# The bonus term of an RWKV layer as a block-diagonal matmul, in a kernel with a written-out order on every engine

## The reference

```python
r = xrg @ Wr.T
k = k * jnp.exp(w * mk)            # k, v, w, kk, a come from low-rank mixes of x
_, y = jax.lax.scan(step, s0, (qt, wt, kt, vt, at, bt))      # the state, token by token
y = ((yg - mu) / jnp.sqrt(var + EPS)).reshape(Bx, Tx, C) * ln_w + ln_b
# the bonus: one number for each token and head, times the head's values
rk = (r.reshape(Bx, Tx, H, HS) * k.reshape(Bx, Tx, H, HS)
      * time_faaaa.reshape(H, HS)).sum(-1, keepdims=True)
y = y + (rk * v.reshape(Bx, Tx, H, HS)).reshape(Bx, Tx, C)
return y * g @ Wo.T
```

## Time and profile before

| | before |
|---|---|
| time, median of 3 runs | 3364.82 us (3361.93 to 3368.27) |
| profiled execution: its own time | 3367.22 us |
| its span, first to last instruction | 3365.5 us |
| granted TensorE clock, mean | 0.977 |
| TensorE busy / weight loads | 2931.0 / 2550.6 us |
| VectorE busy | 2887.9 us |
| ScalarE busy | 1831.5 us |
| GpSimd busy | 1444.6 us |

### The profile page before, as it was taken

One profiled execution on the slowest core, in us unless ns is written; L12 is line 12 of the kernel. 1 busy time (PEld: TensorE's weight loads), 2 busy tenths in 40 slices (PEclk: granted clock), 3 DMA queues, 4 the chain that ended last, 5 costly groups with the idle time before them and its releaser, 6 DMA issues.

```text
span 3365.5 us, 175696 instructions
## 1 busy us (share of the span) xinstructions
PE 2931.0 (87%) x80128; PEld 2550.6 (76%) x80128; DVE 2887.9 (86%) x5699; ACT 1831.5 (54%) x3457; POOL 1444.6 (43%) x1224
## 2 busy tenths in 40 slices
PE   6898888998888989888888888888988889888895
PEld 5777777787777777777777777777777778777774
DVE  4888898898898888898888988888888889889885
ACT  3555564564554555655555645555556556555452
POOL 5344344444353444444443543534434435435332
PEclk8999999999999999999999999999999999999997
DMA  3121221221211212212212212122122122122121
GB/s 115 46 60 38 53 56 36 58 55 36 60 46 45 60 37 53 59 38 53 56 38 56 52 39 60 39 52 60 37 53 56 38 56 56 38 56 48 43 53 36
DMA packets 92604, 170.69 MB, mean 51 GB/s; under 512 B 13908, under 2 KB 14932, under 8 KB 91864
## 3 DMA queue, kind: packets, MB, share of 16 engines
q1 hardware_dynamic: 91864, 159.45, 19.8%
HBM read 41.97 MB, written 16.78 MB: 17 GB/s over the span
## 4 chain that ended last, share of the span: by engine, by line
PE 63%; DVE 27%; issue 8%; DMA 1%; POOL 0%; ACT 0%; SPq 0%; POOLq 0%; DVEq 0%; ACTq 0%
PE bank L1101 22%; PE bank_a L1240 11%; PE bank L1301 8%; DVE stacked L938 4%; PE bank_a L1218 3%; PE bank_b L1218 3%; PE bank_b L1271 3%; DVE kt L859 3%; PE bank_a L1256 3%; PE bank_a L1248 2%; DVE x2n L985 2%; PE bank_b L1291 2%; DVE xm_rg L815 2%; DVE xm_k L815 2%; DVE xm_v L815 2%
## 5 line engine op out<-in xcount | busy, mean ns | idle before, releaser
L474 POOL TENSOR_TENSOR rs<-rs,minus_half 128x1 f32<-128x1 f32 x64 | 35.0, 548 | 1168.1 <-DVE rs L981 1168.1
L676 ACT ACT_TABLE_LOAD x256 | 328.4, 1283 | 4.6
L1240 PE MATMUL bank_a<-pw,w_ffn_int 32*32 32x64 f32 x16384 | 273.3, 216 | 57.3 <-issue 50.7
L1101 PEld LDWEIGHTS bank<-xm_k,w_k 128*128 128x128 f32 x2048 | 236.4, 194 | 107.8 <-issue 107.8
L1101 PE MATMUL bank<-xm_k,w_k 128*128 128x128 f32 x2048 | 246.6, 279 | 79.1 <-DVE xm_rg L815 77.4
L1101 PEld LDWEIGHTS bank<-xm_v,w_v 128*128 128x128 f32 x2048 | 269.6, 204 | 58.8 <-issue 53.1
L1240 PEld LDWEIGHTS bank_a<-pw,w_ffn_int 32*32 32x32 f32 x16384 | 242.9, 106 | 82.9 <-issue 60.4
L1101 PE MATMUL bank<-xm_v,w_v 128*128 128x128 f32 x2048 | 288.0, 291 | 14.2 <-issue 14.1
L1301 PE MATMUL bank<-w_o,yc 128*128 128x512 f32 x512 | 285.9, 663 | 9.3 <-DVE yc L780 9.3
L1101 PE MATMUL bank<-xm_rg,w_r 128*128 128x128 f32 x2048 | 257.6, 279 | 0.8 <-issue 0.7
L1101 PEld LDWEIGHTS bank<-xm_rg,w_r 128*128 128x128 f32 x2048 | 239.1, 192 | 8.2 <-issue 2.3
(11 more groups left out here) (198 smaller groups left out, 8621.9 us busy)
## 6 DMA issues: line engine op xcount, KB each, us to landing
streamed<-aq_state SPq DMA_DIRECT2D x128, 384.0 KB
streamed<-w_ffn_int SPq DMA_DIRECT2D x128, 384.0 KB, 5.3
xin<-in_x SPq DMA_DIRECT2D x128, 128.0 KB
xres<-in_x SPq DMA_DIRECT2D x128, 128.0 KB
out<-o_sb SPq DMA_DIRECT2D x128, 128.0 KB, 2.4
w_ffn_int<-in_weight_q SPq DMA_DIRECT2D x1, 2048.0 KB, 10.7
w_k<-in_Wk SPq DMA_DIRECT2D x1, 1024.0 KB
w_r<-in_Wr SPq DMA_DIRECT2D x1, 1024.0 KB
```

The source lines that it names most:

```text
L676: nc.scalar.preload_act_table_set(functions)
L1101: ins = mm(bank[:, o * n:(o + 1) * n], weights[:, k, o * P:(o + 1) * P], x[:, k].rearrange("p b t -> p (b t)"), start=(k == 0), stop=(k == ...
L1240: ins = mm(bank_a[q, 64 * n:64 * n + 64], pt[q, g, :], source[q, g, 0:2].rearrange("p j t -> p (j t)"), start=True, stop=True)
```

## The change

`w_bonus` is a 128 x 128 matrix for each block of channels, block-diagonal with four 32 x 32 blocks, each row filled with the channel's `time_faaaa`. TensorE multiplies it with `qk`, which sums over the channels of a head and spreads the sum over them in one go, into `fb[3]`; VectorE multiplies that with `val`. `bonus_rows`, `bonus_sums` and the transposition in `bonus` on VectorE, `weighted_bonus` and `bonus_values` on GpSimd are gone. New waits: `values` on ScalarE for `v_rkv` (tile before), `transposed_input` on TensorE for `v_rkv` (it writes `fb[3]`), TensorE's `bonus` for `g_qk` and `a_mk`, GpSimd's `bonus` for `p_bonus`, VectorE's `undecayed` for `a_a`. All four compute engines have a new order; SyncE's is unchanged.

```diff
@@ constants, GpSimd and VectorE
+                then(pool.memset(w_bonus[:], 0.0))
+                for h in range(QH):
+                    then(pool.memset(w_bonus[quad(h), :, quad(h)], 1.0))
...
-            V.transpose(faaaa_T[:], faaaa[:].unsqueeze(2).to_broadcast([P, KB, HS])).then_inc(ffn_done, 1)
             dve.wait_ge(masks_done, 1)
+            for k in range(KB):
+                ins = V.tensor_scalar(w_bonus[:, k], w_bonus[:, k], faaaa[:, k:k + 1], None, ALU.mult)
+            ins.then_inc(ffn_done, 1)
@@ ScalarE
             def values(i):
                 act.wait_ge(p_v, count(i, 1, 1))
                 act.wait_ge(v_vraw, count(i, 1, 0))
+                act.wait_ge(v_rkv, count(i, 1, 0))
@@ VectorE
             def bonus(m):
-                dve.wait_ge(g_rkv, count(m, 1, 1))
+                dve.wait_ge(p_bonus, count(m, 1, 1))
+                dve.wait_ge(a_v, count(m, 1, 1))
                 dve.wait_ge(g_z3, count(m, 1, 0))
-                V.transpose(by_chunk(rkv), qkT[:]).then_inc(v_rkv, 1)
+                tt(rkv[:], fb[3][:], val[:], ALU.mult).then_inc(v_rkv, 1)
@@ TensorE
             def transposed_input(i):
                 pe.wait_ge(a_xn, count(i, 1, 1))
                 pe.wait_ge(a_mk, count(i, 1, 0))
+                if i >= 2:
+                    pe.wait_ge(v_rkv, count(i - 2, 1, 1))
...
+            def bonus(m):
+                pe.wait_ge(g_qk, count(m, 1, 1))
+                pe.wait_ge(a_mk, min(count(m + 1, 1, 1), NT))
+                for k in range(KB):
+                    ins = mm(fb[3][:, k * TOK:(k + 1) * TOK], w_bonus[:, k],
+                             qk[:, k * B * NC:(k + 1) * B * NC].rearrange("p g t -> p (g t)"), start=True, stop=True)
+                ins.then_inc(p_bonus, 1)
```

More of the change, by code:

```diff
@@ L726, in tile_step @@
                 if project:
-                    mk_gate(i)
                     tables(EXP_LN)
+                    log_squares(i)
+                if solve:
+                    power(m, 1)
+                if project:
                     log_sigmoid(i)
[L730 to L734, removed]
                     exponentials(i)
@@ L737, in tile_step @@
                     normalised(j)
+                if solve:
+                    value_pairs(m)
+                    power(m, 2)
+                if mix:
                     front_transposed(j)
                 if project:
+                    key_decay(i)
                     values(i)
+                    queries(i)
+                if mix:
+                    tables(SIGMOID_TANH)
+                    low_rank(j)
                 if solve:
@@ L852, in undecayed @@
             def undecayed(i):
+                dve.wait_ge(a_a, count(i, 1, 1))
                 dve.wait_ge(g_kkp, count(i, 1, 1))
@@ L1034, in tile_step @@
                 if solve:
-                    bonus(m)
-                    power(m, 2)
-                if project:
-                    removal_directions(i)
+                    power(m, 1)
                 if mix:
@@ L1041, in tile_step @@
                 if solve:
-                    half_inverse(m)
-                    right_hand_sides(m, 0)
+                    bonus(m)
+                if project:
+                    removal_directions(i)
+                if solve:
+                    power(m, 2)
                 if project:
@@ L1351, in tile_step @@
                     half_inverse(m)
-                    from_values_and_state(m, 0)
-                if mix:
-                    transposed_input(j)
-                if solve:
-                    inverse(m)
                 if finish:
                     project_out(n, [2])
+                    project_out(n, [3])
                 if project:
@@ L1361, in tile_step @@
                 if solve:
-                    solve_step(m, 0)
-                if finish:
-                    project_out(n, [3])
+                    inverse(m)
+                if mix:
+                    low_rank(j)
                 if project:
@@ L1367, in tile_step @@
                 if solve:
+                    solve_step(m, 0)
+                    output_gate(m)
                     from_solutions(m, 0)
-                if mix:
-                    low_rank(j)
-                if solve:
-                    output_gate(m)
-                    from_values_and_state(m, 1)
                 if mix:
@@ L1376, in tile_step @@
                 if solve:
-                    solve_step(m, 1)
+                    from_values_and_state(m, 1)
                 if finish:
```

138 lines of the change are left out of this document (63 added, 75 removed).

## The result

The changed kernel took 3283.45 us at the median of four runs (3277.99 to 3293.85), the kernel before 3363.38 us beside it: ratio 0.9768, 95% interval 0.9737 to 0.9798. That is 80 us less, where 30 were forecast; it lies in the range, at its fast edge.

A forecast was written before the change was run, and what follows sets the result against it. TensorE (87% busy) and VectorE (86%) were too close to name one; each step chains a stretch of both. 38.7 + 2.8 + 9.3 = 50.8 us against 51.3, over 61 steps -30 us: 3334 us, range 3280 to 3385.

The forecast's parts named there:

- TensorE stretch, work: TensorE's part of each step without gaps: from 35.8 us to 38.7, with bonus +1.0, moved matmuls +2.1, half clock -0.2.
- gaps in it: TensorE's instruction-fetch gaps in small-matmul groups: from 3.2 us a step to 2.7, the inverse's share taken as 0.55.
- VectorE stretch with its gaps: Step's tail from state update to next keys: 9.3 us in place of 12.3, plus 0.1 for gaps newly met there.
- The case of fewer gaps: Rival: TensorE's gaps fall to 2.0 us a step, the step to 50.0, 3286 us; chance 0.16.
- its rival: TensorE's half clock moves into the new tail; at 1.2 us every second step, 51.4 a step, 3371 us; chance 0.12.
- ScalarE late for the gates: Rival: gates behind `scores_b` wait for ScalarE's `kraw`; if 1 us later, step 51.8 us, 3395 us; chance 0.08.
- these 1.4 us: VectorE's removed bonus work, inside the TensorE stretch: worth nothing by itself, useful only as room.
- +2.9 and -3.4: Per step: TensorE work from 35.8 to 38.7 us, against gaps from 3.2 to 2.8 and VectorE stretch from 12.3 to 9.3.

The follow-up runs named there:

- experiment 3: Changed kernel with 13 more idle TensorE instructions a step and 161 once ahead, holding instruction loads at a good place: 3179.17 us, ratio 0.9441.
- 4: Changed kernel with 13 more idle TensorE instructions a step and 118 once ahead, so a load falls in mid-inverse: 3342.38 us, ratio 0.9922.
- Experiment 6: Kernel of experiment 3 with VectorE's `bt` and `kt` back in their old place, between `xm_v` and `xm_rg`: 3332.44 us, ratio 0.9916.
- 7: Kernel of experiment 3 with two unread 128x512 GpSimd products added right behind `norm2_rstd`: 3291.45 us, ratio 0.9796.
- Experiment 1: Kernel before, in its old order, with only the bonus changed to the TensorE matmul: 3472.61 us, ratio 1.0318.
- 13: New order with the old bonus, 17 met instructions in place of the bonus matmuls, and the padding of experiment 3: 3321.43 us, ratio 0.987.
- 14: Kernel of experiment 3 with two VectorE transposes of a constant tile added where the old bonus had its operations: 3225.89 us, ratio 0.9585.
- experiment 9: Kernel before with 30 idle TensorE instructions a step, half before the second solve, half at step end, loads 20 instructions earlier: 3316.53 us, ratio 0.9831.
- experiment 5: Kernel before with 30 idle TensorE instructions a step, all before the second solve, and 186 once ahead: 3423.66 us, ratio 1.0176.

## Why the prediction came out as it did

The direction and the mechanism were right, the size was not: 50.8 us a step were forecast, 49.9 measured.

| term | forecast | measured |
|---|---|---|
| TensorE stretch, work | 38.7 | 38.5 |
| gaps in it | 2.7 | 2.2 |
| VectorE stretch with its gaps | 9.3 + 0.1 | 9.2 |

- *The gaps* are the step that failed, 0.5 of the 0.9 us. Only the inverse was lowered, to 0.55 (measured 34.6 / 58 = 0.60). But `half_inverse`, `from_values_and_state(m, 0)` and the inverse had stood in one row and were all spread out: the first two fell from 0.25 and 0.28 to 0.04 and 0.02. The three powers fell from 1.08 to 0.85. Taking a gap per group "as now" missed that a load's cost depends on how fast the instructions around it run off, for every group; that the gaps are the loads is shown by experiments 3 and 4, that the spreading is what lowered them is argued from the order. In front of the inverse 0.20 is new, VectorE late behind the slow `mix`.
- The case of fewer gaps had a chance of its own (0.16) with 3286 us, and 3283 came. That the two agree so closely is luck: the case had the gaps at 2.0, they came to 2.2, and the work and the VectorE stretch, 0.2 shorter each, made up for it.
- *The work* came out 0.2 lower. The bonus took 1.00, as put. `project_out` took 3.64 in place of 4.01 and the two inverse stages 2.51 in place of 2.78; `gate_hidden` rose from 0.98 to 1.26, since the half clock now falls on it: 135 of its 464 matmuls have it, 231 ns each in place of 126. In all the half clock went from 154 to 140 us, so its rival did not come.
- *The VectorE stretch*: 9.3 was 0.2 too long. `kt`, `x2n` and `bt` took the fast times, and the wait for the state is 0.81 where 0.8 was said. Experiment 6 shows that the move of `bt` and `kt` carries the gain, 7 that it needs GpSimd idle.
- *ScalarE late for the gates* did not happen: the gates wait 1.0 us in the whole run.
- "By themselves these 1.4 us are worth nothing. They pay as room": both halves are shown. Experiment 1 gives the first; experiments 13 and 14 give the second, and show that the room was needed, which the sum of parts did not price: in the new order 1.4 us more on VectorE cost 0.82 a step.
- The forecast was a small difference of large terms (+2.9 and -3.4). An error of 0.9 us in 51 is 2%, but nearly twice the 0.5 us that were forecast as the gain.

## What to carry over

Two halves of a change can each be a loss and the whole a gain: the cheaper operation and the order that uses the freed time are to be priced together. Where one engine runs thousands of tiny instructions in an unrolled program, count them: if a step is a whole number of instruction loads the place of the loads can be chosen, and here that was worth more (104 us, the saved half clock included) than the change itself (80 us). What an engine's idle neighbour does is part of an operation's duration; look for both values of a line (shortest and median) before using its mean.

## What the runs showed of the hardware

- TensorE stood still with all operands there, up to 2.1 us in the inverse and 4.0 at most (in a power), nine gaps in ten ending 2.3 to 2.8 us behind the start of a 16 KB packet of the instruction queue. The gaps lie in groups that run off 256 instructions in 1.2 to 2 us, or in what stands right behind them (`values` behind the last power in experiment 9). The Trainium skill ("Runtime: NRT & Kernel Launch", Instruction fetch mechanics) holds the fetch of instructions for mostly hidden. The two runs that differ in 43 idle instructions and in 163 us contradict it here.
- Some VectorE operations with SBUF inputs alone ran two to four times longer beside a GpSimd product: `kt` 685 and 1529 to 1660 ns, `x2n` 543 and 1176 to 1258, `mix` about 340 and up to 1364. `rkv`, which reads a PSUM bank, did not: 0.68 us in all 64 tiles, in 59 of them beside a GpSimd product. The Trainium skill ("SBUF — State Buffer", Who interferes with whom) says that a VectorE instruction with two SBUF inputs contends with a GpSimd instruction that reads SBUF, that one in a two-port mode contends with GpSimd as well, and that one with at most one SBUF input outside these modes does not. The traces agree for `kt`, `mix` and `rkv`; that `x2n`, with one such input, runs in a two-port mode is shown by no run here.
- A met wait that needs an instruction of its own is not free: 30 of them took 2.5 us, some 84 ns each.
- Where TensorE stood still longer, more half clock (1.2 GHz) followed: before the second solve of experiment 5 it stood 2.5 us in each step, and the clock records show 404 us of half clock, where the kernel before had 154. In the 2780 us of steady steps of experiment 3, with a wait of 0.8 us for the state in each, there was none. Window of experiment 5 behind such a wait, with PEclk 0.59, and the steady steps of experiment 3, with 1.00 (us, busy us by engine, PEclk, DMA share, GB/s):

```profile
1789.00:1792.40 3.40, 3.23 (x40) 3.12 (x41) 3.39 (x6) 0.60 (x2) 1.80 (x2) 0.59 0.00 0
```

```profile
222.96:3003.13 2780.17, 2643.97 (x73083) 2329.39 (x73082) 2491.43 (x5047) 1657.83 (x3132) 1113.55 (x928) 1.00 0.22 53
```
